# Attention block with stacked high and low parts of q: the high parts' copies issued ahead of the low part's

## What is computed

```python
def xattn(hidden, enc, Wq, Wk, Wv, Wo, gq, bq, gk, bk):   # H = 16 heads of 32
    q, k, v = heads(hidden @ Wq), heads(enc @ Wk), heads(enc @ Wv)
    q = layernorm(q, gq, bq)                               # over the 32 of a head
    k = layernorm(k, gk, bk)
    attn = softmax(einsum('bhqd,bhkd->bhqk', q, k) / sqrt(32))
    return merge(attn @ v) @ Wo

def reference(x, ctx, ...):                                # x (2, 2048, 512), ctx (2, 128, 512)
    x = x + xattn(layernorm(x), ctx, ...)
    s = layernorm(x) @ Win + bin_                          # (.., 64)
    g = einsum('btmh,mh->btm', relu(s[..., None] * W1 + b1), W2) + b2
    return x + g @ Wout + bout
```

## Time and profile before

| | |
|---|---|
| median of three runs | 536.48 us (536.0 to 541.8) |
| the profiled execution | 536.35 us, of it a span of 534.6 us from first to last instruction |
| mean granted TensorE clock | 0.970 of 2.4 GHz |
| TensorE matmuls | 474.9 us busy, 89% |
| VectorE | 409.6 us, 77% |
| ScalarE | 266.6 us, 50% |
| GpSimd | 184.5 us, 35% |
| DMA queue of SP | 57.60 MB, 40.9% of 16 engines |

### The profile page before, as it was taken

One profiled execution on the slowest core, in us unless ns is written; L12 is line 12 of the kernel. 1 busy time (PEld: TensorE's weight loads), 2 busy tenths in 40 slices (PEclk: granted clock), 3 DMA queues, 4 the chain that ended last, 5 costly groups with the idle time before them and its releaser, 6 DMA issues.

```text
span 534.6 us, 7294 instructions
## 1 busy us (share of the span) xinstructions
PE 474.9 (89%) x2352; PEld 307.8 (58%) x2352; DVE 409.6 (77%) x744; ACT 266.6 (50%) x487; POOL 184.5 (35%) x166
## 2 busy tenths in 40 slices
PE   1879869999999999989999999999988978986666
PEld 1456644775578567846586658755864436534532
DVE  6799857988898889978897899788877695543622
ACT  1245438517851776148633883288316840762142
POOL 6232542831443134402551165205623530304120
PEclk9899989999999999999999999999999999997967
DMA  8502883183137512591069014910680077104002
GB/s 289 166 21 52 229 195 90 60 210 88 41 117 181 138 41 75 162 216 42 25 204 209 21 39 168 219 31 0 152 241 6 1 161 206 29 1 137 20 0 78
DMA packets 25109, 58.32 MB, mean 109 GB/s; under 512 B 5744, under 2 KB 6256, under 8 KB 22000
## 3 DMA queue, kind: packets, MB, share of 16 engines
q1 hardware_dynamic: 24816, 57.60, 40.9%
q10 hardware_dynamic: 256, 0.26, 0.2%
HBM read 22.20 MB, written 8.39 MB: 57 GB/s over the span
## 4 chain that ended last, share of the span: by engine, by line
PE 61%; DVE 12%; DMA 11%; SPq 6%; ACT 4%; issue 4%; POOL 1%; ACTq 0%; DVEq 0%
PE bank L1554 29%; PE bank L1648 6%; DMA q_stack<-mxt 6%; PE bank L1560 6%; PE bank L1636 6%; PE bank L1692 5%; PE bank L1616 4%; PE bank L1651 3%; DMA q_stack<-qt_hi 2%; DVE mx L697 1%; SPq L248 1%; ACT hid L1243 1%; DMA s_in<-in_L_ffn_Win_dram 1%; DVE z L739 1%; POOL at_lo L463 1%
## 5 line engine op out<-in xcount | busy, mean ns | idle before, releaser
L1196 ACT ACTIVATE prob<-bank 128x512 f32<-128x512 f32 x128 | 72.6, 600 | 46.0 <-PE bank L1636 34.4
L697 DVE TENSOR_REDUCE mx<-bank 128x4 f32<-128x512 f32 x128 | 80.6, 677 | 10.0 <-PE bank L1616 9.9
L458 POOL TENSOR_TENSOR qt_lo<-u,qt_hi 128x512 fp32r<-128x512 f32 x32 | 42.9, 1345 | 84.9 <-DVE u L688 84.9
L471 POOL TENSOR_TENSOR x<-x,bout_row 128x512 f32<-128x512 f32 x32 | 43.4, 1376 | 77.7 <-DVE z L739 77.7
L453 POOL TENSOR_TENSOR rden<-u 128x512 f32<-128x512 f32 x32 | 34.9, 1091 | 83.4 <-DVE ssq L675 41.5
L1648 PE MATMUL bank<-prob,v_kv 128*32 128x512 f32 x256 | 63.3, 601 | 0.0
L1651 PE MATMUL bank<-prob,den_sel 128*32 128x512 f32 x256 | 62.7, 601 | 0.0
L1636 PE MATMUL bank<-q_stack,k_stack 97*128 97x512 f32 x128 | 47.8, 446 | 13.3 <-DMA q_stack<-mxt 12.6
L463 POOL TENSOR_TENSOR at_lo<-att,at_hi 128x512 fp32r<-128x512 f32 x32 | 40.4, 1286 | 46.6 <-ACT at_hi L1222 46.6
L1554 PE MATMUL bank<-wo_hi,at_hi 128*128 128x512 f32 x128 | 52.3, 409 | 3.9 <-POOL at_lo L463 3.9
L1554 PE MATMUL bank<-wq_hi,zt_hi 128*128 128x512 f32 x128 | 52.7, 411 | 3.3 <-DVE zt_lo L669 3.3
(11 more groups left out here) (129 smaller groups left out, 964.0 us busy)
## 6 DMA issues: line engine op xcount, KB each, us to landing
q_stack<-qt_hi SPq DMA_DIRECT2D x64, 256.0 KB, 5.6
xin<-in_x_dram SPq DMA_DIRECT2D x32, 256.0 KB, 2.7
q_stack<-qt_lo SPq DMA_DIRECT2D x32, 256.0 KB, 5.3
x<-in_x_dram SPq DMA_DIRECT2D x32, 256.0 KB, 3.1
out_dram<-x SPq DMA_DIRECT2D x32, 256.0 KB, 2.6
x<-in_L_xattn_Wq_dram SPq DMA_DIRECT2D x4, 256.0 KB, 6.7
att<-in_L_xattn_Wk_dram SPq DMA_DIRECT2D x1, 1024.0 KB, 9.2
hid<-in_L_xattn_Wv_dram SPq DMA_DIRECT2D x1, 1024.0 KB, 10.5
```

The lines of the kernel that those rows point to most:

```text
L458: pool.tensor_tensor(qt_lo[:, :, cols], u[:, j, :].rearrange("p (i n) -> p i n", i=HC), qt_hi[:, :, cols].bitcast(F32), ALU.subtract).then ...
L471: pool.tensor_tensor(x1[:, j, :], x1[:, j, :], bout_row[:, :], ALU.add).then_inc(bout_added, 1)
L697: dve.tensor_reduce(mx[:, j, :].rearrange("p (g i) -> p i g", g=G)[:, i, :], maxs_bank[T][i][j][:, :].rearrange("p (g n) -> p g n", g=G), ...
L1196: act.activation(prob[:, h % PR, :], score_bank[t][h][:, :], ACT.Exp, scale=SCALE).then_inc(exp_done, 1)
```

## The change

In `stack_q` the first wait of a block is for the high parts in place of the low ones. The copies of a group go out in the order part 0 (high), part 2 (high), part 1 (low). In group 0 the wait for the low parts stands directly ahead of the copy of part 1. The wait for the scores of the block before is where it was, the copies have the same sources, destinations and semaphores, and all other lists are unchanged.

```diff
             def stack_q(T, gr):
 
                 if gr == 0:
-                    sp.wait_ge(qt_lo_done, T * TB + TB)
+                    sp.wait_ge(qt_hi_done, T * TB + TB)
                 if not first(T):
                     sp.wait_ge(scores_done, T * H + (gr + 1) * HC - H)
                 rows, heads = slice(HD * gr, HD * (gr + 1)), slice(HC * gr, HC * (gr + 1))
-                for part, src in enumerate((qt_hi, qt_lo, qt_hi)):
+                for part, src in ((0, qt_hi), (2, qt_hi), (1, qt_lo)):
+                    if gr == 0 and part == 1:
+                        sp.wait_ge(qt_lo_done, T * TB + TB)
                     sp.dma_start(q_stack[HD * part:HD * (part + 1), heads, :].bitcast(F32),
                                  src[rows, :, :].bitcast(F32)).then_inc(stacked[gr], 16)
```

## The result

The changed kernel is slower. Over 22 executions of each, taken in turn on one chip, the medians are 541.5 us (537.4 to 546.2) and 538.6 us before (531.1 to 545.7), and the ratio is 1.0088 with a 95% interval of 1.0059 to 1.0118, that is 3.2 to 6.4 us. The forecast was 536.3 and a range up to 538.8: too low, and on the side of "no change" where the loss is just under 1%. Of the 5.2 us between the forecast's 536.3 and 541.5, 2.1 are the kernel before itself, whose median was 536.5 in the three runs that the forecast started from and is 538.6 here.

What follows compares the result with a forecast made beforehand. TensorE (busy 89% of the span) and VectorE (77%) were read as busiest, DMA mattering only where it ends a wait. From 536.35: minus 0.1 (block 0), 0 (blocks 1 to 7), 0 (order) gives 536.3 us, range 533.8 to 538.8.

Steps and rivals of the forecast that it cites:

- The change does what it says: Blocks 0 and 7: high copies go at 57.5, 58.1 and 420.3, low ones at 59.6 and 427.7; extra checks cost 0.2 us.
- Block 7, gain 0: Two high copies go at 420.3 instead of 427.7, but scores wait for the maxima's copy: gain 0, at most 1.1 us.
- The order costs nothing: Within each group, parts going 0, 2, 1 instead of 0, 1, 2 were taken to cost 0, bounded by +-2.5 us.
- The rival that gave it 2.5 us: The order costs: new copy order in the groups adds 2.5 us, giving 538.8; chance 0.07.
- the rule on ports: Partitions 0 to 63 and 64 to 127 use separate port halves; by it the new order could cost up to 2.5 us.
- A copy handed over 2 us sooner stands 2 us longer in line: Block 0: DMA engines are full from 58 to 76, so two earlier copies gain only 0.1 us.
- in line behind it as well: Block 0, argument against Win landing later: before the change, the copies of 59.58 also stood behind Win.
- Win comes later: Block 0, slower rival: two early copies move Win's landing from 63.21 to 65.7, +2.5 us, 538.8; chance 0.08.
- the rival of the head start: Block 0: burst and maxima's copy come sooner, TensorE waits 1.9 us less, clock saves 1.7; 3.6 us, 532.7; chance 0.15.

Runs made afterwards that it cites:

- e4: The whole change in blocks 1 to 7, block 0 as before, against the kernel before: 535.1 us beside 537.5, ratio 0.9976 (0.9944 to 1.0008).
- e2: Kernel before with only the order of the three copies changed, in all blocks: 536.3 us beside 537.5 before, ratio 0.9980 (0.9936 to 1.0025).
- e9: Changed kernel plus 16 unread matmuls in each of TensorE's two idle times of block 0: 538.5 us beside 538.9 before, ratio 1.0051.
- e1: The changed kernel again, unaltered, against the kernel before on another comparison's chip: 541.3 us beside 537.5, ratio 1.0116 (1.0078 to 1.0154).
- e3: New waits and new order in block 0 alone, blocks 1 to 7 as before: 541.3 us beside 537.5 before, ratio 1.0086 (1.0048 to 1.0124).
- e8: Kernel before, old order, but a block's first copy waits only for the high parts: 541.9 us beside 536.9 before, ratio 1.0068 (1.0019 to 1.0116).
- e5: Changed kernel plus a wait until Wo and Win have landed before block 0's first copy of q: 536.1 us beside 536.9 before, ratio 1.0002.
- e12: Changed kernel with Wo and Win loaded early and 16 unread matmuls in both idle places: 533.6 us beside 538.9 before, ratio 0.9906.
- e7: Changed kernel with the loads of Wo and Win moved ahead of the first keys' copies: 532.6 us beside 536.9 before, ratio 0.9984.
- e10: Kernel before with the loads of Wo and Win moved ahead of the first keys' copies: 535.4 us beside 538.9 before, ratio 0.9965.

## Why the prediction was wrong

Step by step, as it was put:

- *"The change does what it says"*: right, in both blocks with a wait. The extra checks of semaphores show nowhere.
- *Block 7, gain 0*: right. The two high copies go out 7.4 us ahead of the low one, SP is through with group 1 at 438.2 and waits for VectorE until 442.5, as it did before. e4, which has this part and not block 0, is level with before.
- *The order costs nothing*: right as far as e2 can tell, whose interval ends at 0.25% or 1.3 us slower. The rival that gave it 2.5 us falls, and with it the use that was made of the rule on ports.
- *"A copy handed over 2 us sooner stands 2 us longer in line"*: this is the step that failed, a cost put at nothing: -0.1 us for block 0, where the profiled pair shows 6.8 by block 1. It took a DMA share of 1.00 as a line in which order of issue decides and the rate is given. The share was as full afterwards, the rate 14% lower in the first 8 us, and the load in front was not protected by having been issued first. The sentence that spoke against the slower rival, that the copies of 59.58 were "in line behind it as well", overlooked the 2.6 us between the two issues, in which no copy of q stood behind Wo and Win yet.
- *"Win comes later"*, rival with a chance of 0.08: the right mechanism. Its price for Win, 2.5 us, was near (2.2 us, and 1.0 to 2.2 over the profiles with two early copies). Its price for the time was too low, since it carried the delay one for one to the end. Three terms were left out: the clock's fall after the longer idle time, 1.8 us up to the issue of the maxima's copy (4.0 - 2.2, and e9 gives it back); the later landing of this copy, 1.5 us; and 1.3 us more up to block 1 (6.8 - 5.5), a stretch in which the scores run at the lower clock for longer. The last of them may be scatter: from the landing of the maxima's copy to block 1's first copy it took 32.2 us before and 33.5 in the changed kernel, but 33.8 in e2, which loses nothing. The ledger from Win's issue is 6.8 us in the profiled pair and 4.3 to 5.7 in e1, e3 and e8. The prediction had priced the clock in the other direction, as a gain in the rival of the head start (1.7 us), and not here.
- *The chance.* The rival hung on a path with no cover: ScalarE was known to wait for Win and for nothing else. Anything done to the queue in front of such a landing should have weighed more than 0.08.

## What to carry to other kernels

Before a DMA is issued sooner, look at what is still under way on the same engines and who waits for its landing: here two copies, 2 us sooner, delayed the one load on the path, and a change that was to remove a wait lost 0.9%. A full DMA share says that there is no room, but not that what stands in front is safe. Where the engine that waits is TensorE, look at the granted clock behind its idle times before you price a longer one: here the lower level cost another 1.4 to 1.8 us.

## What was not expected of the hardware

**The end of the run comes at different speeds.** The profiled executions of the same changed kernel end at 541.9 us and, in e1, at 530.5. Of these 11.4 us, 6.05 are there when block 7's maxima are issued (454.65 and 448.60); the rest comes after that. The stage from 505 to 525 us, first in the kernel before:

```profile
505.00:525.00 20.00, 14.60 (x44) 7.41 (x44) 5.82 (x8) 9.04 (x13) 5.56 (x4) 0.66 0.00 0
```

in e1:

```profile
505.00:525.00 20.00, 11.87 (x48) 6.48 (x49) 6.28 (x12) 9.51 (x14) 5.57 (x4) 0.91 0.00 0
```

and in e5:

```profile
505.00:525.00 20.00, 13.07 (x54) 7.33 (x54) 6.38 (x10) 9.52 (x14) 5.04 (x4) 0.93 0.00 0
```

From the issue of block 7's maxima to the end it takes 87.4 us in the profile of before and 87.2 in that of after, but 81.9, 81.8, 81.8 and 81.5 in e1, e3, e5 and e8, all four with a granted clock of 0.91 to 0.93 in this stage. The ten other profiles have 84.4 (e12) to 89.1 us (e7) and 0.59 to 0.74. What decides between them isn't known. One profile of each kernel doesn't compare their ends; stages of the same work do.

**An idle time's length alone does not tell the clock.** TensorE came out of idle times of 2.1 and 2.3 us before max_scores at full clock in e2 and in the kernel before, while in e4 the clock fell 1.6 us after an idle time of 2.3 us. After the 3.5 us and more that it was idle there in e8, e1, e3 and the changed kernel it was at 0.50. Before the first scores a shorter idle time in e10 was followed by a fall (its row of 72 to 76 us stands above) and a longer one in e4 was not. First e10:

```profile
71.22 1.17 PE L1636 MATMUL bank<-q_stack,k_stack 97*128 97x512 f32 x4 [2.19 <-DMA q_stack<-mxt]
```

then e4, with the stage behind it:

```profile
75.58 0.70 PE L1640 MATMUL bank<-q_stack,k_stack 97*128 97x512 f32 x2 [2.62 <-DMA q_stack<-mxt]
...
76.00:80.00 4.00, 4.00 (x26) 1.61 (x24) 1.35 (x5) 3.76 (x9) 0.00 (x0) 1.00 0.55 131
```

**Full engines, less moved.** In the 8 us from Wo's issue the engines moved 236 to 255 GB/s at a share of 0.95 to 1.00 where one or two copies from SBUF to SBUF were issued right behind the loads (after, e3, e8, e9), and 277 to 282 at 0.97 to 1.00 where the first came 2.6 us later (before, e2). With no copy of q at all, in the first 5.5 us of e5, they moved about as much at a lower share:

```profile
56.10:61.60 5.50, 5.50 (x25) 4.25 (x24) 5.50 (x10) 1.09 (x2) 3.55 (x3) 1.00 0.85 273
```
